# Two head groups searched for row maxima beside the projections, and attention's order set anew

## The reference, cut to what matters

```python
q, k, v = (proj(wq), proj(wk), proj(wv))      # 32 heads of 16 numbers each
q = _apply_rope(q, sin, cos)
k = _apply_rope(k, sin, cos)
scores = jnp.einsum('bnth,bnsh->bnts', q, k) * (1.0 / math.sqrt(h))
scores = jnp.where(causal, scores, -jnp.inf)
attn = jax.nn.softmax(scores, axis=-1)
out = jnp.einsum('bnts,bnsh->bnth', attn, v)
```

## Time and profile before

| what | value |
|---|---|
| median of three runs | 855.82 us |
| the profiled execution | 856.97 us, span 855.3 us |
| PE busy over the span | 789.7 us (92%) |
| DVE busy | 633.4 us (74%) |
| ACT busy | 428.6 us (50%) |
| POOL busy | 304.5 us (36%) |
| granted TensorE clock, mean | 0.971 |

### The profile page before, as it was taken

How to read it: one execution, slowest core, us unless ns; L and a number is a source line. 1 busy time by engine, 2 the same in 40 slices (tenths; PEclk the granted TensorE clock), 3 DMA queues, 4 the chain that set the end, 5 groups by cost and what they waited for, 6 DMA issues and landing times.

```text
span 855.3 us, 18978 instructions
## 1 busy us (share of the span) xinstructions
PE 789.7 (92%) x7930; PEld 375.8 (44%) x7930; DVE 633.4 (74%) x895; ACT 428.6 (50%) x576; POOL 304.5 (36%) x217
## 2 busy tenths in 40 slices
PE   8568697887999999999999999999998999999997
PEld 2434344444544444444334444444435544444444
DVE  3999999998556434456748999999976787774344
ACT  3885657564854331143225777787784633332100
POOL 0599899994103000058410222212233222221000
PEclk9599999999999999999999999999998999999999
DMA  6900000005321000039800000000231023320001
GB/s 200 382 13 3 3 3 2 3 4 172 99 84 34 1 0 1 1 55 191 148 1 2 2 2 1 2 2 2 51 131 62 1 80 129 127 84 0 13 37 50
DMA packets 53297, 46.63 MB, mean 55 GB/s; under 512 B 38290, under 2 KB 44242, under 8 KB 53219
## 3 DMA queue, kind: packets, MB, share of 16 engines
q1 hardware_dynamic: 53218, 45.49, 18.6%
HBM read 34.87 MB, written 2.16 MB: 43 GB/s over the span
## 4 chain that ended last, share of the span: by engine, by line
PE 72%; DVE 15%; issue 5%; POOL 4%; ACT 3%; DMA 1%; SPq 1%; DVEq 0%; POOLq 0%; ACTq 0%
PE ps L880 13%; PE ps L632 10%; PE ps L655 10%; DVE arena L1407 8%; PE ps L803 7%; PE ps L916 7%; PE ps L734 6%; PE ps L711 6%; PE ps L787 3%; POOL arena L1257 3%; PE ps L738 2%; DVE arena L1633 2%; PE ps L546 2%; PE ps L502 1%; ACT arena L1163 1%
## 5 line engine op out<-in xcount | busy, mean ns | idle before, releaser
L1633 DVE TENSOR_REDUCE arena<-ps 128x1 f16<-128x512 f32 (+3 forms) x320 | 182.8, 631 | 16.1 <-PE ps L738 8.2
L1163 ACT ACTIVATE arena<-ps 128x1024 f32<-128x1024 f32 (+2 forms) x160 | 142.3, 942 | 46.3 <-PE ps L787 45.4
L1257 POOL TENSOR_TENSOR arena<-arena 128x1024 f32<-128x1024 f32 x62 | 152.0, 2486 | 9.4 <-DVE arena L1407 8.9
L1407 DVE TENSOR_TENSOR_SCAN arena<-arena,ps 128x1024 f32<-128x1024 f32 x64 | 142.0, 2270 | 1.4 <-PE ps L546 1.1
L880 PE MATMUL ps<-arena 128*128 128x512 f16 x528 | 114.6, 379 | 0.1
L734 PE MATMUL ps<-arena 64*128 64x512 f16 (+3 forms) x384 | 97.7, 329 | 2.8 <-DVE arena L1640 1.2
L655 PE MATMUL ps<-arena 128*128 128x512 f16 (+1 forms) x464 | 97.6, 372 | 1.0 <-ACT arena L1081 1.0
L1006 ACT ACTIVATE arena<-arena,negA 128x1024 f32<-128x1024 f32 x64 | 72.9, 1146 | 45.2 <-DVE arena L1407 43.4
L1307 POOL TENSOR_SCALAR_AFFINE_SELECT arena<-arena 128x512 f32<-128x512 f32 x64 | 42.4, 669 | 145.6 <-ACT arena L1163 145.5
L546 PE MATMUL ps<-arena 64*128 64x64 f16 x3072 | 60.5, 196 | 35.8 <-DVE arena L1407 32.2
L546 PEld LDWEIGHTS ps<-arena 64*128 64x128 f16 x3072 | 52.6, 99 | 86.4 <-DVE arena L1407 78.5
(11 more groups left out here) (173 smaller groups left out, 966.4 us busy)
## 6 DMA issues: line engine op xcount, KB each, us to landing
arena<-in_w_q_dram SPq DMA_DIRECT2D x11, 768.0 KB, 4.3
arena<-c_rows SPq DMA_DIRECT2D x16, 512.0 KB, 11.8
arena<-in_w_s_dram SPq DMA_DIRECT2D x11, 384.0 KB, 4.8
arena<-in_x_fm_dram SPq DMA_DIRECT2D x8, 256.0 KB, 4.7
out_dram<-arena SPq DMA_DIRECT2D x8, 256.0 KB, 2.0
arena<-in_wg_dram SPq DMA_DIRECT2D x1, 1792.0 KB, 9.8
arena<-in_wu_dram SPq DMA_DIRECT2D x1, 1792.0 KB, 7.3
arena<-in_wd_dram SPq DMA_DIRECT2D x1, 1792.0 KB, 11.3
```

What stands on the lines that cost most here:

```text
L1163: nc.scalar.activation(dst, src, ACT.Exp, scale=float(HD) ** -0.5).then_inc(exp_done, 1)
L1257: nc.gpsimd.tensor_tensor(hC[i % 4][:], hst[i % 3][:], c_all[:, n, :], ALU.mult).then_inc(hc_done, 1)
L1407: nc.vector.tensor_tensor_scan(hst[i % 3][:], dA[i % 3][:], banks(2 * (i % 2), 2), 0.0, ALU.mult, ALU.add).then_inc(scan_done, 1)
L1633: nc.vector.reduce_max(maxima_slot(half, k), ps[:, ring_bank(n), 0:len(heads) * w].rearrange("p (a w) -> p a w", a=len(heads)), AX, negate ...
```

## The change

1. **Group 1 is searched beside the projections too.** `EARLY_PLAN` is one list for PE and DVE that holds quarters of projections (3 matmuls), searches of groups 0 and 1, the turns of the maxima and the first two keys. Before, whole or half projections stood between pairs of searches. Now one search stands behind each quarter while q and k are projected (from token tile 3), and two behind each quarter of a value projection. 80 units stand there instead of 40, in 55 places instead of 20; attention keeps 240 of 280.
2. **The maxima's buffers are doubled** (`m_b`, `m_neg` by the group's parity), and their small copies for group 1's first half are written to `q_st` at the end of the stage (`put_rows`, in SP's queue behind the last tile's transposes).
3. **Banks.** Values of even tiles go to bank 3 and of odd ones to bank 7, so that bank 2 joins the ring from the 37th search on (`PAIRED`).
4. **The second mask matmul has 64 columns instead of 128** (the other half of its mask holds only zeros), in all 8 groups.
5. **Attention's string is new.** The first group's keys are followed by searches at once; before, two pairs of keys and two values steps stood first. Searches beside the keys of groups 0 to 6 number 39, 35, 37, 33, 29, 34 and 31; before, 38, 41, 37, 40, 40, 40 and 43. PE changes between searches or keys and another kind of work 222 times, before 236.

```diff
-            return ((4, 5, 7), (6, 3, 2))[t % 2][w]
+            return ((4, 5, 3 if t else 7), (6, 2, 7))[t % 2][w]
...
-        m_b = view(199.25, 4 * GH, f16).rearrange("p (i a) -> p i a", i=4)
-        m_neg = [view(199.5 + h / 8, 4 * GH, f16).rearrange("p (i a) -> p i a", i=4) for h in range(2)]
+        m_b = [view(199.25 + u / 8, 4 * GH, f16).rearrange("p (i a) -> p i a", i=4) for u in range(2)]
+        m_neg = [[view(199.5 + u / 8 + h / 16, 4 * GH, f16).rearrange("p (i a) -> p i a", i=4) for h in range(2)] for u in range(2)]
...
-        EARLY_TILES = TT
-        EARLY_UNITS = [(half, k) for i in range(EARLY_TILES) for half in range(2) for k, unit in enumerate(SEARCH[half]) if unit[0] == i]
-        EARLY_TURN = len(max_units(0)) + 2
-        EARLY_UNITS.insert(EARLY_TURN, None)
-        EARLY = len(EARLY_UNITS)
+        EARLY_GROUPS = 2
         LEAD = 3
-
-        def early_units(t, place):
-
-            units = [n for n, unit in enumerate(EARLY_UNITS) if unit is not None and SEARCH[unit[0]][unit[1]][0] == t - LEAD]
-            if len(units) == 2:
-                return units if place else []
-            return ([EARLY_TURN] if (t, place) == (TT - 1, 1) else []) + units[2 * place:2 * place + 2]
-        BEHIND = [n for n in range(EARLY) if n > max(early_units(TT - 1, 1))]
-        BESIDE_VALUES = [BEHIND[at:at + 2] for at in range(0, len(BEHIND), 2)]
-
-        def maxima_slot(half, k):
+        AHEAD = 2
+
+        def early_plan():
+
+            plan = [("project", 2, 0, c) for c in range(DC)]
+            ready = []
+
+            def tile(i):
+                return [("search", g, half, k) for g in range(EARLY_GROUPS) for half in range(2)
+                        for k, unit in enumerate(SEARCH[half]) if unit[0] == i]
+            for t in range(1, TT):
+                for w in range(2):
+                    for c in range(DC):
+                        if t >= LEAD and (w, c) == (0, 2):
+                            ready += tile(t - LEAD)
+                        plan.append(("project", w, t, c))
+                        plan += ready[:1]
+                        del ready[:1]
+                        if (t, w, c) == (TT - 1, 0, DC - 1):
+                            plan.append(("turn", 0, 0))
+            for at in range((TT - 1) * DC):
+                if at % DC == 0 and at // DC in (0, 1, 3):
+                    ready += tile(TT - LEAD + (0, 1, 3).index(at // DC))
+                if at == (TT - 1) * DC - 2:
+                    plan += [("keys", 0, 0, 0, (u,)) for u in range(AHEAD)]
+                plan.append(("project", 2, 1 + at // DC, at % DC))
+                plan += ready[:2]
+                del ready[:2]
+                if at == 3:
+                    plan.append(("turn", 1, 0))
+            return plan + ready + [("negate", 0, 1), ("turn", 0, 1)]
+        EARLY_PLAN = early_plan()
+
+        def in_ring(steps):
+            return [step for step in steps if step[0] in ("search", "turn", "out")]
+        EARLY = len(in_ring(EARLY_PLAN))
+        PAIRED = len(in_ring(EARLY_PLAN[:EARLY_PLAN.index(("project", 2, 1, 2))])) // 2 * 2 + 2
+
+        def maxima_slot(g, half, k):
 
             i, key, _, heads = SEARCH[half][k]
-            dst = m_b[:, i - 4, :] if key else m_neg[i // 4][:, i % 4, :]
+            dst = m_b[g % 2][:, i - 4, :] if key else m_neg[g % 2][i // 4][:, i % 4, :]
             r, b = heads[0]
             return dst[:, b:GH:2] if len(heads) == 2 else dst[:, 2 * r + b:2 * r + b + 1]
 
...
         MASK_TO = list(itertools.accumulate(int(on_diagonal(half, j)) for _, half, j in STEPS))
         RING = 3
 
-        HEAD = ("kknntkkvkvsskssssssvssvsksskokssksskssksnsksvtskssvsskksvssksvskkssvssks"
...
+        ATTENTION = ("kknsssskskssskkssvskkssvssksskvsvssnskksvssksksvsskksvssvsksskvsktsksvssksksvsvsskksosvssksvskks"
...
-                "s": iter([("search", g, half, k) for g, half in halves for k in range(len(SEARCH[half]))
-                           if g or (half, k) not in EARLY_UNITS]),
-                "n": iter([("negate", g, half) for g, half in halves]),
-                "t": iter([("turn", g, half) for g, half in halves if g or half]),
+                "s": iter([("search", g, half, k) for g, half in halves if g >= EARLY_GROUPS for k in range(len(SEARCH[half]))]),
+                "n": iter([("negate", g, half) for g, half in halves if ("turn", g, half) not in EARLY_PLAN]),
+                "t": iter([("turn", g, half) for g, half in halves if ("turn", g, half) not in EARLY_PLAN]),
...
-            for letter in HEAD + 3 * PATTERN + TAIL:
+            for letter in ATTENTION:
...
+        IN_RING = in_ring(EARLY_PLAN) + in_ring(ORDER)
+        RING_AT = {step: n for n, step in enumerate(IN_RING)}
...
-            return n % 2 if n < EARLY else (n - EARLY) % RING
+            return n % 2 if n < PAIRED else (n - PAIRED) % RING
+
+        def ring_before(n):
+
+            return next((o for o in range(n - 1, -1, -1) if ring_bank(o) == ring_bank(n)), None)
...
-                if t == TT - 2:
-                    put_rows(0, 0)
+                if t >= TT - 2:
+                    put_rows(t - (TT - 2), 0)
...
-                if EARLY <= n < EARLY + RING:
-                    pe.wait_ge(ring_read, EARLY)
-                elif n >= EARLY + RING:
-                    pe.wait_ge(ring_read, n - RING + 1)
-                elif n >= 2:
-                    pe.wait_ge(ring_read, n - 1)
+                before = ring_before(n)
+                if before is not None:
+                    pe.wait_ge(ring_read, before + 1)
+                else:
+                    pe.wait_ge(roped, 2 * TT if ring_bank(n) == 2 else 1)
                 return ring_bank(n)
...
-                        for s in range(2):
-                            last = nc.tensor.matmul(dst[:, w - P:w], picks_b[rows, s, :], mask_b[rows, s, :], start=False, stop=(s == 1))
+                        for s, cols in ((0, P), (1, SUB)):
+                            last = nc.tensor.matmul(dst[:, w - cols:w], picks_b[rows, s, :], mask_b[rows, s, P - cols:P], start=False, stop=(s == 1))
...
+            def project_part(w, t, c):
+
+                if c == 0 and w == 2 and t:
+                    pe.wait_ge(v_kept, max(t - 1, 1))
+                elif c == 0 and w < 2 and t >= 2:
                     pe.wait_ge(roped, 2 * (t - 2) + w + 1)
...
+                elif c == 0 and w < 2:
...
+                project(w, xh, xl, t, qkv_bank(t, w), (q_proj, k_proj, v_proj)[w] if c == DC - 1 else None, (c,))
...
-            value(0)
-            for t in range(1, TT):
-                for w in range(2):
-                    query_or_key(w, t)
-                    for n in early_units(t, w):
-                        early(n)
-            for at, pair in enumerate(BESIDE_VALUES):
-                for n in pair:
-                    early(n)
-                t, part = divmod(at, 2)
-                if t + 1 < TT - 1:
-                    value(t + 1, range(part * DC // 2, (part + 1) * DC // 2))
-            pe.wait_ge(roped, 2 * TT)
-            for e in range(AHEAD):
-                keys(*ORDER[e][1:], e)
-            value(TT - 1)
+            e = 0
+            for kind, *at in EARLY_PLAN:
+                if kind == "project":
+                    project_part(*at)
+                elif kind == "search":
+                    early_search(*at, RING_AT[kind, *at])
+                elif kind == "turn":
+                    turn_maxima(*at, RING_AT[kind, *at])
+                elif kind == "keys":
+                    pe.wait_ge(roped, 2 * TT)
+                    pe.wait_ge(v_kept, TT - 1)
+                    keys(*at, e)
+                    e += 1
             pe.wait_ge(v_kept, TT)
             e = AHEAD
             for kind, g, half, *at in ORDER[AHEAD:]:
...
                     turn_out(g, half, RING_AT[kind, g, half])
...
+            rope(0, 0)
+            rope(1, 0)
+            for kind, *at in EARLY_PLAN:
+                if kind == "project" and at[0] < 2 and at[2] == DC - 1:
+                    rope(*at[:2])
+                elif kind == "search":
+                    maxima(*at, RING_AT[kind, *at])
+                elif kind == "negate":
+                    negate(*at)
+                elif kind == "turn":
+                    keep_rows(*at, RING_AT[kind, *at])
 
```

More of the change, by code:

```diff
@@ L276, in build @@
         ORDER = attention_order()
-        AHEAD = 2
-        IN_RING = [step for step in ORDER if step[0] in ("search", "turn", "out")]
-        RING_AT = {step: EARLY + n for n, step in enumerate(IN_RING)}
-        RING_AT["turn", 0, 0] = EARLY_TURN
+        IN_RING = in_ring(EARLY_PLAN) + in_ring(ORDER)
+        RING_AT = {step: n for n, step in enumerate(IN_RING)}
         def searched(g, half):
-            if (g, half) == (0, 0):
-                return len(SEARCH[0])
-            return max([RING_AT["search", g, half, k] for k in range(len(SEARCH[half])) if ("search", g, half, k) in RING_AT],
```

(36 more changed lines are left out.)

33 lines of the change are left out of this document (7 added, 26 removed).

## The result

The changed kernel took a median of 861.93 us (four runs, 860.08 to 862.07), the kernel before 854.53 us beside it (852.98 to 855.97): a ratio of 1.0089, 95% interval [1.0071, 1.0106]. That is 7.4 us slower where 1.7 us faster was forecast. The profiled executions, 860.08 and 856.97 us, differ by only 3.1 us, because the kernel before reached this stage 4.0 us later in its one (371.2 us against 367.2), through stages that the change does not touch. So I compare stage by stage (the number before each comma is the length of a stretch): from the first value projection (token tile 0) to the end of the last, then attention to its last search, then the tail to the first transposition of its output.

The account below looks back on a forecast made before the run. PE was taken to bound both projections and attention, DVE just below in attention. 15.8 - 8.8 - 4.0 - 2.9 - 3.0 + 1.2 = -1.7 us gave 855.3 against the profiled 856.97, so 854.1 us in the metric; range 845 to 862.

Parts of the forecast that it names:

- Term 1: Beside the projections: searches +10.0 us, interruptions +8.0, the first turn's waits gone -2.2; sum +15.8 us.
- two banks behind a rope: Rival, between tiles 3 and 7: searches wait for banks while DVE stands at a rope for POOL; +6 us, chance 0.13.
- Term 2: Attention: one group's searches leave it, 11.3 us x 0.78 = -8.8 us.
- Term 3: Attention: narrower masks of the 6 groups left there, 192 x 0.027 x 0.78 = -4.0 us.
- Term 4: Hand-over to attention: searches following the turn at once remove most waits and slow first values steps, -2.9 us.
- Term 5: Attention: PE waits less for DVE's maxima, above all at the start; -3.0 us.
- Term 6: Attention: new waits as ACT's load rises to 81% in a shorter period, +1.2 us.
- 78%: Attention: share of the search and mask time leaving the stage that was said to come off the end.
- DVE as the real bound: Rival, attention: DVE bounds it, so 40 maxima less give 22.8 us; total -13.5, 842.3 us; chance 0.16.
- ACT's chain: Rival, attention: ACT's chain holds the period, groups 0 to 6 take 23.9 us instead of 22.3; 865 us, chance 0.12.
- The narrow mask: Rival: the narrow mask gives nothing, 4.0 + 1.7 us back, 859.8 us; chance 0.09.
- The sign for the ropes: Beside the projections: matmul waits on DVE over 2 us would show the forecast wrong.

Follow-up runs that it names:

- the parts together: Kernel before with attention's new start, the 64-column mask and the first turn of the maxima two searches later: 850.89 us, 0.9935 of the kernel before.

## Why the prediction was wrong

**Term 1, searches beside the projections: +20.0 us instead of +15.8.** The failed step is that DVE "still has room", with waits for a bank put at nothing and the old stall's 2.2 us taken off in full. The old stall did go (at the first turn 0.42 us are left), but six waits of about 4.3 us came, in place and kind mostly the rival "two banks behind a rope" (+6, chance 0.13). With two banks a search needs its bank back after two quarters and the search between them: the unit of 383.30 ends near 383.7 and PE is ready for its bank at about 385.6, some 1.9 us later. A rope alone takes 1.26 us and fits, as the ropes at 404.56 and 409.03 show; with 0.79, 1.06 or 1.60 us for POOL before it, it does not, and these are the three waits of 0.37, 0.67 and 0.86 us. The rival had said this, from 0.4 us of waiting on. The argument against it, that a longer tile gives POOL's chain time, came true only from 404 us on. The three later waits answer to the words "now a projection quarter stands between any two", which are not so at the turn and behind value quarters: there PE is back at the bank after one quarter, some 1.1 us (418.5 to 419.6), less than a rope. I had looked at DVE's sum over the stage (59 of 72 us) and not at the longest stretch in which it frees no bank. The rest of the term held: 15.8 and 4.3 make 20.1, against 20.0 measured, and with the third bank, where one wait is left, the stage grew by 16.2. So +10.0 for streaming and 35 x 0.23 us for interruptions were right. The 3.2 us more that the Trainium skill's lone-matmul latency ("TensorE: Matmul & The Clock Gate", "Single matmul latency") would have given as an estimate are not there: with them, 15.8 would be 19.0, against the 16.2.

**Where attention stood: "PE is at its bound, and DVE just below".** This is the second failed step, and terms 2 to 5 rest on it. DVE cost attention about 6.6 us before. I had excluded that by 0.3 us of waiting matmuls and by the weight load that "idled under a running matmul". The load did idle under a matmul, but the covered time of the searches suggests that its own search could often have run beside that one, on the other half of the rows.

**Terms 2 to 6: -12.2 us instead of -17.5.** By the pieces that runs separate:
- Term 3 (masks, -4.0) measured -2.6 in attention, half of the full price of 5.2 and not 78% of it.
- Term 4 (hand-over, -2.9): the new start alone gave -3.2 on the kernel before, and in the changed kernel PE stood 0.59 us behind the turn (461.88, for ACT), where the sum had left some 0.4. The number is near, in part by luck: 1.3 us of it were values steps at half clock, and the run with halved maxima shows the old order without them. That share belongs to one execution of the kernel before.
- Term 5 (DVE's lateness, -3.0): it did not shrink. 6.6 us became 7.5.
- Term 6 is not what is missing: half of ACT's work gave 0.5 us.

Terms 3 and 5 were thus wrong by 1.4 and 3.9 us, which is the 5.3 that are missing; a profile is one execution, and this fit is no closer than about 1 us. Term 2 was not measured by itself. With the maxima halved in both kernels attention up to the last search shrank by 11.1 us, where terms 2 to 4 without the clock's 1.3 us have 14.4 and term 6 takes 1.2 back; the masks' 1.4 us are most of the difference. The 78% itself was read from a period of 25.03 us that held some 0.9 us of DVE's lateness; with that taken off, my estimate would have been 71%.

Why a DVE that is free 10% of the time still costs 7.5 us is open: it had 24.2 us for some 34 searches a group, and reads them in the order in which PE can issue them between keys and values. Only one other spacing was run, the old one, and it was worse by 7.8 us.

**The net sign.** 4.2 us too little in term 1 and 5.3 too much in the others turn -1.7 into +7.8; less 0.7 us of the stages behind, 7.1. Of the two causes the missing bank alone explains 4.5 us of the slower time; with the third bank the kernel lies at +0.35%, within my "same".

**The rivals.** DVE as the real bound was true of 6.6 us of the old attention and false in its consequence (842.3 us): it held PE in part, before and after. ACT's chain fell by the halved exponentials, though its sign of being wrong did show: loads before keys stood 8.4 us for ACT, over the 5 named. A weight load's wait was again no measure of the end. The narrow mask gives 4.0 us in the changed kernel, not nothing. The sign for the ropes, over 2 us of waits, came with 3.23. DVE's share in attention was said to fall under 97%, and did (90%); the stage was called wrong over 75 us from the first search, and took 78.6 (382.16 to 460.8), 3.2 of it because the first search stands 15 projection matmuls earlier than in the kernel before.

## What to carry to other kernels

An engine that is busy all the time can still be held up, where its instructions are able to run side by side: halve the other engine's work and look at the end time and at the covered time of the instructions, not at idle time or at the waits of weight loads. Look at the granted clock of both profiles before the difference is called the other engine's. Before work is spread between an engine's other duties, compare the number of buffers with the longest stretch in which the reader does something else, not with its mean load. And work that left a stage where two engines were full took less with it here than either engine's share.

## What the runs showed of the hardware

The granted clock fell after a stall in some executions and not in others, with the same instructions and waits before it. Five profiles have the old projection stage, one of them with a later turn. In two (the kernel before and that with the narrow mask) the clock fell at the hand-over, behind 0.69 and 1.24 us of idle PE; in three (new start, halved maxima, and the parts together) it fell behind the first turn, and the hand-over ran at full clock, in that with halved maxima behind the same 0.69 and 1.24 us. The projection stage of the run with the new start is that of the kernel before, with the same stall of 1.22, 0.23 and 0.28 us. In it the clock then was, by stretch:

```profile
416.30:419.60 3.30, 3.02 (x8) 0.82 (x7) 1.61 (x3) 1.04 (x1) 2.35 (x3) 0.54 0.52 99
```

and in the kernel before:

```profile
416.60:420.00 3.40, 2.65 (x13) 0.97 (x14) 2.60 (x5) 1.04 (x1) 3.36 (x3) 1.00 0.59 110
```

Six projection matmuls took 2.74 us in the one, where 1.47 is usual: at 1.2 GHz instead of 2.4, and 1.3 us lost. The stage was 75.1 us there instead of 73.6. A stall can thus cost more than its idle time, here 1.3 to 1.5 us more, and a single profile may not show it, or may show it in another place.
